# Row weights at every second partition, and row groups loaded in the order 0, 2, 1, 3

## The reference

```python
om = conv3x3(x, w_off) + b_off                  # 27 planes: 9 y offsets, 9 x offsets, 9 masks
py = off_y + row + ky;  px = off_x + column + kx
y0, x0 = floor(py), floor(px);  wy, wx = py - y0, px - x0
sampled = (v00*(1-wy)*(1-wx) + v01*(1-wy)*wx + v10*wy*(1-wx) + v11*wy*wx) * sigmoid(mask)
out = einsum('bckhw,ock->bohw', sampled, w) + b
out = relu(batchnorm(out)) + x
```

## Time and profile before

| | |
|---|---|
| median of 3 runs | 2611.33 us (2609.78 to 2625.12) |
| the profiled execution | 2600.78 us |
| its span, first to last instruction | 2599.1 us |
| mean granted TensorE clock over it | 0.804 of full speed |
| bytes moved by DMA, mean rate | 362.95 MB, 140 GB/s |
| sampling stage | about 670 to 2370 us of the span |

### The profile page before, as it was taken

One profiled execution on the slowest core, in us unless ns is written; L12 is line 12 of the kernel. 1 busy time (PEld: TensorE's weight loads), 2 busy tenths in 40 slices (PEclk: granted clock), 3 DMA queues, 4 the chain that ended last, 5 costly groups with the idle time before them and its releaser, 6 DMA issues. The chain is left out here.

```text
span 2599.1 us, 71650 instructions
## 1 busy us (share of the span) xinstructions
PE 1630.6 (63%) x24206; PEld 1099.0 (42%) x24207; DVE 1563.4 (60%) x1718; ACT 1452.1 (56%) x2219; POOL 624.6 (24%) x1168
## 2 busy tenths in 40 slices
PE   5567920000188787877877878778787787884340
PEld 5442310000165565555645556455564554553220
DVE  5260036667187686866867768667586686776114
ACT  2122243332187686876867768667686686783002
POOL 2000000000243332422333234233342332421000
PEclk9688965555599898988988889888898898997555
DMA  2277836666786776756766667576576775762007
GB/s 104 65 196 200 242 113 245 247 247 233 183 134 138 132 126 116 144 118 113 133 131 123 119 117 140 123 125 120 109 138 121 136 127 113 137 125 46 3 0 304
DMA packets 288911, 362.95 MB, mean 140 GB/s; under 512 B 61852, under 2 KB 260819, under 8 KB 285013
## 3 DMA queue, kind: packets, MB, share of 16 engines
q1 hardware_dynamic: 209552, 226.57, 39.9%
q0 software_dynamic: 36864, 59.94, 13.2%
q10 hardware_dynamic: 42182, 72.05, 8.1%
HBM read 253.94 MB, written 104.39 MB: 138 GB/s over the span
## 5 line engine op out<-in xcount | busy, mean ns | idle before, releaser
L790 PE MATMUL ps_odd_y<-rows,sel 32*128 32x504 f32 (+2 forms) x928 | 483.6, 521 | 602.5 <-DMA rows<-scratch_parts 355.7
L750 POOL DMA_DIRECT2D rows<-scratch_parts x1152 | 601.0, 523 | 1069.3 <-PE ps_even_y L781 963.4
L930 DVE TENSOR_TENSOR G<-odd_y,ps_odd_v 128x1008 f32<-128x1008 f32 (+2 forms) x464 | 541.9, 1168 | 327.2 <-PE ps_odd_v L807 325.8
L807 PE MATMUL ps_even_v<-tent_x,stage 32*128 32x171 f32 (+2 forms) x5568 | 573.8, 336 | 88.9 <-issue 84.1
L807 PE MATMUL ps_odd_v<-tent_x,stage 32*128 32x171 f32 (+3 forms) x5568 | 592.3, 330 | 0.0
L886 ACT COPY even_v<-ps_even_v 128x1008 f32<-128x1008 f32 (+2 forms) x464 | 450.7, 971 | 235.3 <-PE ps_odd_v L807 234.7
L880 ACT COPY odd_y<-ps_odd_y 128x504 f32<-128x504 f32 (+2 forms) x928 | 525.6, 566 | 70.4 <-PE ps_odd_y L790 65.2
L938 DVE TENSOR_TENSOR G<-even_v,ps_even_y 128x1008 f32<-128x1008 f32 (+2 forms) x464 | 539.0, 1162 | 2.6 <-PE ps_even_y L781 1.9
L790 PEld LDWEIGHTS ps_odd_y<-rows,sel 32*128 32x128 f32 x928 | 182.7, 197 | 809.5 <-ACT odd_y L880 415.8
L825 PE MATMUL ps_r<-G,conv_w 128*32 128x224 f32 (+1 forms) x8832 | 522.8, 367 | 1.9 <-issue 1.2
L807 PEld LDWEIGHTS ps_even_v<-tent_x,stage 32*128 32x128 f32 x5568 | 470.1, 200 | 93.4 <-issue 88.0
(11 more groups left out here) (134 smaller groups left out, 909.5 us busy)
## 6 DMA issues: line engine op xcount, KB each, us to landing
place<-scratch_px SPq DMA_DIRECT2D x960, 105.0 KB, 3.5
scratch_parts<-parts ACTq DMA_DIRECT2D x18, 3136.0 KB, 16.7
rows<-scratch_parts POOLq DMA_DIRECT2D x960, 52.5 KB, 4.0
x<-scratch_xh SPq DMA_DIRECT2D x48, 406.0 KB, 6.0
place<-scratch_px SPq DMA_DIRECT2D x192, 84.0 KB, 4.0
scratch_om<-om ACTq DMA_DIRECT2D x64, 196.0 KB, 7.0
rows<-scratch_parts POOLq DMA_DIRECT2D x192, 42.0 KB, 4.1
scratch_conv<-res SPq DMA_DIRECT2D x448, 14.0 KB, 2.1
```

What stands on the lines that cost most here:

```text
L750: pool.dma_start(sub(rows[b], 32 * g, Y_KINDS, here, [[GROUP * W, 3], [1, count * W]]).bitcast(fp32), dram("parts", there, [[PLANE, Y_KIND ...
L790: nc.tensor.matmul(ps_odd_y[:, lo:hi], sel[32 * g:32 * g + 32, :], taps(rows, 32 * g, 32, p, lo, hi), start=True, stop=True).then_inc(odd_ ...
L807: m = nc.tensor.matmul(sub(ps_v[g // 2], 0, 128, i * 512 + lo + first, dims), stage[32 * g:32 * g + 32, j * IMAGE + v * C:j * IMAGE + (v + ...
L930: nc.vector.tensor_tensor(two(G, ROW, v, slot(v)), two(odd_y[p % 3], ROW, v), two(ps_v[1], 512, v), ALU.mult).then_inc(odd_weighted, 1)
```

## The change

Two things change, and nothing else.

- The 16 kinds of a group lie at partitions 32g, 32g+2, ..., 32g+30, not at 32g to 32g+15. `load_rows` writes with a partition step of 2, and `sel` has its ones in the even rows: kind k is at partition 2k of the group, so that its window row is (p // 2) % 8.
- The loops over the row groups are turned round in `load_place`, `load_rows` and `load_stage`. The groups now come in the order 0, 2, 1, 3. In `load_place` and `load_rows` each still has its three tap rows in turn; in `load_stage` the column range is now the outer loop, and the group changes with each DMA.

Number, size and sources of the DMAs, and all waits, are as before.

```diff
                 def load_place(pair, n):
                     first, count = BATCHES[n]
                     b = n % 2
-                    for parity in range(2):
-                        for i in range(2):
+                    for i in range(2):
+                        for parity in range(2):
                             g = 2 * parity + i
                             for ky in range(3):
...
                 def load_stage(pair, c):
                     first, count = BANDS[c]
-                    for g in range(4):
-                        for j, (x0, lo, hi) in enumerate(COLUMNS):
+                    for j, (x0, lo, hi) in enumerate(COLUMNS):
+                        for g in (0, 2, 1, 3):
...
                 def load_rows(pair, n):
                     first, count = BATCHES[n]
                     b = n % 2
-                    for parity in range(2):
-                        for i in range(2):
+                    for i in range(2):
+                        for parity in range(2):
                             g = 2 * parity + i
...
-                                pool.dma_start(sub(rows[b], 32 * g, Y_KINDS, here, [[GROUP * W, 3], [1, count * W]]).bitcast(fp32),
+                                pitch = rows[b][:].ap[0][0]
+                                pool.dma_start(bass.AP(tensor=rows[b][:].tensor, offset=32 * g * pitch + here,
+                                                       ap=[[2 * pitch, Y_KINDS], [GROUP * W, 3], [1, count * W]]).bitcast(fp32),
                                              dram("parts", there, [[PLANE, Y_KINDS], [HW // 2, 3], [1, count * W]])
                                              ).then_inc(rows_loaded[b], 16)
...
-    out["sel"] = ((p[:, None] % 32 < Y_KINDS) & (p[:, None] % WIN == m[None] // C)).astype(f)
+    out["sel"] = ((p[:, None] % 2 == 0) & (p[:, None] // 2 % WIN == m[None] // C)).astype(f)
```

## The result

The changed kernel takes 2511.71 us (median of 4, 2507.76 to 2514.85), the kernel before, beside it, 2612.36 us (2609.78 to 2625.12). The ratio is 0.9605, with a 95% interval of 0.957 to 0.9639: 100.6 us less, where 67 us were forecast (2544 us, with 2510 as the lower end of the range). The profiled execution of the changed kernel took 2514.85 us, its span is 2513.2 us. Against the span of before (2599.1) that is 85.9 us. Of the other 15 us, 11.6 come from the kernel before, whose profiled execution (2600.8) was one of its fastest, and 3.1 from the changed kernel, whose profiled execution was the slowest of its four.

The account below looks back on a forecast made before the run. Late place loads were taken to hold up PE, ACT and DVE, which wait on each other. Gains of 49 us mid-pair, 15 at turns and 3 at the start, 67 in all, took 2611 to 2544 us; range 2510 to 2612.

Parts of the forecast that it names:

- the term for the turn: Between pairs, ACT's wait for place batch 0 shrinks by 1.0 us at each of 15 turns: 15 us.
- What bounds the kernel: Sampling stage: no engine is full; PE, ACT and DVE wait on each other, and late place loads add 138.9 us.
- the ring of PE, ACT and DVE: Sampling stage, 700 to 2400 us: these three engines wait on each other in a circle; largest entry 414.9 us.
- Kinds at every second partition: Rows loads beside place: spreading partitions brings a batch's last place landing from 7.8 to 5.2 us, at no POOL cost.
- Mid-pair, 49 us: Inside pairs, away from turns: 80% of 61 us goes, made of 45.7 us place waits and 15 us clock loss.
- the clock dip: After long place waits inside a pair, the granted clock falls to 0.66 on average: 14 x 1.1 = 15 us.
- Start, 3 us: First samples wait 4.8 us for stage behind place and 24 rows DMAs; 3 us of it goes.
- Order: Group order 0, 2, 1, 3 on SP and POOL: worth 0, as both queues stay about in phase.
- Nothing changes: Rival: two queues sharing an engine, or HBM reads, set the 182 GB/s; 2611 us, give or take 5; chance 0.22.
- POOL pays: Rival: POOL's rows DMAs take 0.2 us more each for stepped partitions; 48 us slower, 2659 us; chance 0.07.
- The backlog goes altogether: Rival: groups 0 and 2 really overlap, 86 us gained, 2525 us, or 2510 if SP issues faster; chance 0.18.
- The base: Starting time for the 67 us: profiled run 2600.8 us gives 2534; median 2611 us gives 2544.

Follow-up runs that it names:

- the kernel with three buffers: The changed kernel with the old stage order, plus a third buffer each for rows and place, loaded a batch earlier: 2427.22 us.
- the layout alone: The kernel before with kinds at every second partition and all three load loops in their old order: 2507.57 us, ratio 0.9622.
- three-buffer pair: Third rows and place buffers, loaded a batch earlier: changed kernel with old stage order, 2427.22 us; kernel before with neighbouring partitions, 2451.5 us.
- place two steps earlier: The changed kernel with old stage order, SP loading place two steps earlier, once ACT's distance has read the buffer: 2476.3 us.

## Why the prediction was right or wrong

**The step that failed** is the term for the turn. It let only the flight of place batch 0 shrink, by 1.0 us at each of 15 turns, and put PE's gap behind the loop's jump back at nothing. The runs showed the reverse: the waits for place batch 0 fell by 5.0 us in all (93.2 to 88.2), and that gap by 19.4 (84.1 to 64.7). Term by term, 67 us were forecast, 49 + 15 + 3, and the profiled spans gave 85.9: mid-pair 55, turns 25.6 in pairs 1 to 14, start 2, and some 3 elsewhere. The medians add 15 us, from the base.

**What bounds the kernel: right.** Late place loads hold the ring of PE, ACT and DVE, and the undisturbed step is 2.95 us; in the kernel with three buffers nearly every step away from the turn keeps to it. That the partitions written held down the 182 GB/s is shown by the layout alone.

**Kinds at every second partition: right, for the layout alone.** I put the last landing of the batch at 5.2 us, halfway between 7.8 and 2.5. With the layout alone the slowest place DMA of that batch takes 5.2 us (4.9 on average over pairs 1 to 14, where it was 7.0), and nearly the whole mid-pair loss is gone with it: steps 8 to 26 exceed the pace by 0.5 us a pair, not 4.6. That it hit so closely is luck, since the lower end was misread: 2.5 us is the median of place alone, and its last one took 3.4. The changed kernel comes to 3.6, because the order speeds up the packets too, which I had denied. I had argued that rows and place still share 16 engines, but at the rates of the earlier trace rows, 17.3 and 14.6 GB/s, a pair of DMAs, one place and one rows of 107.5 and 53.8 thousand bytes, needs 107.5 / 17.3 + 53.8 / 14.6 = 9.9 us of engine time, or 0.62 us on 16 engines, about POOL's issue interval of 7.17 / 12 = 0.60. The engines were hardly short.

**Mid-pair, 49 us: about right.** Steps 8 to 26 give 3.6 us a pair, 14 x 3.6 = 51, and the last pair 4.7 more. The waits of batches 2 and 4 and the clock dip behind them are gone, as said. Part came back in steps 10 to 17 (0.37 to 0.95 us a pair): place batch 3, which had been late in 4 pairs for 5.5 us in all, is now late in 11 for 12.9, since the steps reach it sooner.

**Turn, 15 us: wrong term, 25.6 us measured** in pairs 1 to 14 (23.3 over all 15 turns). I expected 1.0 us less wait for place batch 0. The wait itself fell only from 6.2 to 5.9 us. Place landed 1.1 us sooner after its first issue (9.3 against 10.4), but SP began 0.8 us later, after the slower stage band. What did shrink is a term that was not in my sum: step 28, 1.35 us a pair. There PE waits with no cause shown ("issue"), 84.1 us in all before and 64.7 after, at the 13 turns at which the loop jumps back. Step 28 exceeds the pace by 8.1 to 10.5 us at these turns, and by 1.2 and 1.5 us at the two turns outside the loop. The three-buffer pair shows that this gap grows with slower loads (108.0 and 93.0 us, and nothing else differs but the layout and the group order). My reading is that PE fetches the loop's instructions there, and that these packets share the DMA engines with the loads. The traces speak for it. In all 26 gaps of the kernel before, a packet of 16 KB on q8, the queue named "instruction", ends inside the gap, 1.3 to 2.6 us before PE goes on. In the three-buffer kernels the q8 packets that start in a gap or just before it take 1.6 us each with the old layout and 1.5 with the new. One gap of the kernel before, and q8 within it (1106.1 to 1109.8 us):

```profile
1109.87 0.43 PE L807 MATMUL ps_even_v<-tent_x,stage 32*128 32x57 f32 x1 [3.79 <-issue]
```

```profile
q8 instruction: 1, 0.02, 3.0%
```

No run changed the instructions alone, so the cause stays argued.

**Start, 3 us:** 8.1 us came at the first step, and 6.0 went back in pair 0. The trace shows why:

```profile
703.47 11.22 SPq L692 DMA_DIRECT2D place<-scratch_px  x24
```

```profile
712.25 0.71 ACT L873 ACTIVATE dist_x<-place,at 128x504 f32<-128x504 f32 x1 [6.33 <-DMA place<-scratch_px]
```

SP issues place batch 1 of pair 0 behind 48 stage loads, at 703.5 us in the changed kernel and 703.7 before. It landed at 712.2 and 712.9. The steps that began 8.1 us earlier now wait for it 6.33 us, where nothing waited before.

**Order: wrong.** I took 0, and said that both queues stay in phase. Alone the order gives 55 us, and mixed at every DMA 89. The Trainium skill (SBUF — State Buffer, section "Can I just issue two DMAs to hit both halves?"), on which I leaned, has only 6% for two DMAs at once to partitions 0 and 64; it is not borne out by these short crowded loads from two queues, whose packets in batch 2 went from 10.5 to 13.2 GB/s. For the time of the changed kernel the 0 did no harm, since the layout alone takes 102 us.

**Rivals.** "Nothing changes" and "POOL pays" are out: 510 ns an instruction. "The backlog goes altogether", at 2525 down to 2510 us and given 0.18, is what the landings of the changed kernel show, and the time is near its lower end. But its way to that end was another: SP issues no faster (6.58 us for place batch 0 in pair 4 against 6.96, 6.65 for batch 2 against 5.87), the turns gave their time in the gap, and the layout alone, with landings of 5.2 us, takes no longer. So its size was in good part luck. Its conditions could have been weighed higher, since the whole of the mid-pair loss hangs on landings that need to be only 2 us sooner.

**The base.** Against its own profiled execution the prediction gave 2534 us and 2514.9 came. The medians moved 15 us more, because the kernel before is slower in most runs than in the profiled one (2597 to 2625 us over all runs), while the changed one keeps within 7 us.

## What to carry to other kernels

When several loads run side by side and the DMA share is near 1 while the GB/s are low, compute MB over busy engine time for each queue alone and together. Here it fell from 17.3 to 10.1 GB/s and from 14.6 to 10.5; such a fall says that the loads collide, and a change of which partitions a load writes (every second, or alternate halves from DMA to DMA) needed no more DMAs or bytes here. Then ask what the slowness costs: here three quarters of it was lateness, and one more buffer gave 160 us with the crowded layout untouched. Fix the lead first, then the layout. Parts of a change that free the same wait do not add up: 102 and 55 us made 101.

## What the runs showed of the hardware

- A load of 16 packets of 3.4 KB to 16 neighbouring partitions slows not only itself but also the other queue's 32-partition loads beside it. Spreading it to every second partition, and nothing else, took rows from 10.9 to 13.0 GB/s per busy engine over the whole kernel, and place beside it in batch 2 from 10.5 to 13.2. With the new order as well, place comes to 17.3, what it has alone.
- Such loads gain if groups below and above partition 64 alternate: 40 us for one queue in blocks of three, 55 for both, 89 with a change at every DMA. With the partitions spread, the order gives no time, and shifting one queue against the other cost some 7 us at most, too little to tell from nothing, though place's packets went from 17.3 to 14.6 GB/s.
- The rule that fits the layout's runs is the port map of the Trainium skill (SBUF — State Buffer, section "Door 1: The DMA port swizzle"). It has 16 neighbours on 4 ports and every second of 32 on 8. The runs agree in that spreading one DMA helps (102 us) and moving it to the other 16 neighbours hardly does (12.7 us). Its estimate in the prediction, a quarter less time for a batch, is near the 13.2 to 10.4 us that batch 2 took from the first issue of place to the last landing (means of 14 pairs). This does not test it: 10.4 us is about SP's issue time and one landing (6.65 + 3.6), and the order has a part in it; with the layout alone it is 11.2.
- PE's gap where the loop jumps back is not fixed: 61 to 108 us in these kernels, over 26 gaps at 13 turns. It is shorter where the loads around it are faster, and it grew from 61.4 to 93.6 us when the wait for place ahead of it went (place two steps earlier).
